# Adding h2 to x2 with a DMA that GpSimd issues, in place of a VectorE instruction, in a two-layer graph network kernel

## The reference

```
h  = relu(layernorm(x))
score = sum(h[src] * h[dst]);  a = softmax of score over the edges of one dst
agg = segment_sum((h @ W_conv + b_conv)[src] * a, dst)
r   = relu(h @ W_res + b_res)
x2  = x + batchnorm(agg + r)                     # layer 1 with its residual
h2 = relu(layernorm(x2))
m  = gelu(gelu([h2[src], h2[dst], edge_attr] @ W_m1 + b_m1) @ W_m2 + b_m2)
boxes = segment_sum(m, dst)
out = x2 + h2 + gelu(gelu([h2, boxes] @ W_c1 + b_c1) @ W_c2 + b_c2)
```

## Time and profile before

| what | value |
|---|---|
| median of 3 runs | 2105.99 us (2104.59 to 2109.98) |
| span of the profiled execution, first to last instruction | 1817.9 us |
| time around the span (median less span) | 288.1 us |
| TensorE busy, in the span | 1463.3 us (80%) |
| VectorE busy | 1485.5 us (82%) |
| GpSimd busy | 1129.4 us (62%) |
| ScalarE busy | 849.3 us (47%) |
| mean granted clock of TensorE | 0.851 of full speed |

### The profile page before, as it was taken

The page is one execution under the profiler, slowest core; times in us unless marked ns, Lnnn a source line. Parts: engine busy times, 40 slices in busy tenths (PEclk is TensorE's granted clock), DMA queues, the critical chain, the costliest instruction groups (busy, mean ns, idle before and its releaser), DMA issues.

```text
span 1817.9 us, 22722 instructions
## 1 busy us (share of the span) xinstructions
PE 1463.3 (80%) x6619; PEld 980.4 (54%) x6619; DVE 1485.5 (82%) x2772; ACT 849.3 (47%) x1497; POOL 1129.4 (62%) x989
## 2 busy tenths in 40 slices
PE   3465556488888888588988988889599999999993
PEld 2133233367777777366656666666345555555541
DVE  8799999688988887798899789888268788788781
ACT  4477777322233222365666566665123433434341
POOL 7777788777777777787500000868756776434446
PEclk9788897667777777797899689888789999999996
DMA  7467664777754333344444434555344453343410
GB/s 232 156 219 229 210 212 157 245 249 261 269 200 130 120 108 110 120 169 159 153 151 165 143 142 163 179 181 174 115 114 146 129 150 106 112 129 101 123 52 17
DMA packets 139616, 286.41 MB, mean 158 GB/s; under 512 B 31154, under 2 KB 48379, under 8 KB 139496
## 3 DMA queue, kind: packets, MB, share of 16 engines
q1 hardware_dynamic: 107176, 254.36, 41.1%
q0 software_dynamic: 32320, 30.62, 7.4%
HBM read 164.51 MB, written 121.80 MB: 157 GB/s over the span
## 4 chain that ended last, share of the span: by engine, by line
PE 48%; DVE 29%; issue 11%; POOL 4%; ACT 4%; DMA 3%; SPq 0%; DVEq 0%; POOLq 0%; ACTq 0%
PE banks L1400 7%; DVE stat L697 5%; PE banks L1390 5%; PE banks L1454 4%; DVE stat L705 4%; PE banks L1321 3%; PE banks L1477 3%; PE banks L1475 3%; PE banks L1484 2%; DVE sums L780 2%; PE banks L1304 2%; DVE xc L711 2%; PE banks L1448 2%; POOL agg_ring L577 2%; PE banks L1372 2%
## 5 line engine op out<-in xcount | busy, mean ns | idle before, releaser
L577 POOL DMA_INDIRECT agg_ring<-agg_rows,edge_idx x196 | 234.6, 1197 | 331.4 <-DMA edge_agg<-agg_ring 270.1
L581 POOL DMA_INDIRECT out<-agg,put_last x196 | 207.6, 1059 | 167.1 <-DVE agg L976 109.9
L577 POOL DMA_INDIRECT x_ring<-in_x,edge_idx x200 | 239.8, 1199 | 63.3 <-issue 60.9
L581 POOL DMA_INDIRECT agg_rows<-agg,put_first x196 | 229.2, 1169 | 59.7 <-issue 57.9
L577 POOL DMA_INDIRECT gout<-in_x,edge_idx x192 | 217.1, 1130 | 58.5 <-issue 57.3
L1400 PEld LDWEIGHTS banks<-packed,cT 96*128 96x128 f32 (+1 forms) x1568 | 202.4, 207 | 43.3 <-issue 42.0
L1400 PE MATMUL banks<-packed,cT 96*128 96x64 f32 (+1 forms) x1568 | 208.8, 291 | 0.0
L1265 PE MATMUL banks<-ident,xc 128*128 128x128 f32 (+1 forms) x784 | 131.4, 316 | 94.1 <-DVE xc L711 94.1
L1265 PEld LDWEIGHTS banks<-ident,xc 128*128 128x128 f32 (+1 forms) x784 | 110.5, 165 | 147.1 <-DVE xc L711 107.7
L1274 PE MATMUL banks<-hT,packed 128*128 128x512 f32 (+1 forms) x196 | 126.8, 781 | 76.3 <-ACT hT L1031 76.3
L1390 PE MATMUL banks<-hT,packed 64*96 64x512 f32 (+1 forms) x392 | 128.5, 735 | 46.4 <-ACT cT L1131 40.8
(11 more groups left out here) (153 smaller groups left out, 3135.9 us busy)
## 6 DMA issues: line engine op xcount, KB each, us to landing
xt<-in_x SPq DMA_DIRECT2D x96, 512.0 KB, 4.2
r_rows<-rT SPq DMA_DIRECT2D x48, 512.0 KB, 5.9
xe<-edge_x SPq DMA_DIRECT2D x96, 256.0 KB, 4.6
agg_rows<-rb SPq DMA_DIRECT2D x48, 512.0 KB
rT<-r_rows SPq DMA_DIRECT2D x48, 512.0 KB, 5.6
out<-xt SPq DMA_DIRECT2D x48, 512.0 KB, 2.6
edge_r<-rr SPq DMA_DIRECT2D x48, 256.0 KB, 3.9
rr<-edge_r SPq DMA_DIRECT2D x48, 256.0 KB, 4.8
```

Source lines behind the costliest of these rows:

```text
L577: A.indirect_dma_start(to, None, table[:, :], bass.IndirectOffsetOnAxis(ap=idx, axis=0), bounds_check=limit, oob_is_err=False).then_inc(si ...
L581: A.indirect_dma_start(table[:, :], bass.IndirectOffsetOnAxis(ap=idx, axis=0), rows_of, None, bounds_check=limit, oob_is_err=False).then_i ...
```

## The change

The VectorE instruction of `add_h2` goes. In its place GpSimd issues, for each step, a plain DMA from SBUF to SBUF that adds: it reads xc and adds it to xt. GpSimd's order is written anew: 36 groups are scattered first; then each step's add is followed by one group, a scatter for the steps 0 to 12 and a gather of group s - 13 from step 13 on. B_y now counts the landings of these DMAs, with three semaphores, one for each buffer of xc. SyncE's schedule of stash_agg follows: up to group a - 14 in the round of pass 3 that has a = 2i, where before it was up to 3 (i - 16).

```diff
+PUTS_AHEAD = 36
-        B_y = stage("x2_plus_h2")
+        B_y = slots("h2_added_to_x2", CS)
...
-                    sp.wait_ge(B_y.sem, B_y.after(S - 1))
+                    B_y.all_done(sp, S)
...
-                due = min(G, max(stashed, 3 * (i - 16)))
+                due = min(G, max(stashed, a - 1 - G + PUTS_AHEAD))
...
+            def add_h2(s):
+                p = nodes_of(s)
+                pool.wait_ge(B_h.sem, B_h.after(s))
+                A.dma_start(xt[s % XS][0:p, :], xc[s % CS][0:p, :], accum_op=ALU.add).then_inc(B_y.of(s), 16)
...
-            for n in range(G):
+            for n in range(PUTS_AHEAD):
                 put_agg(n)
-            G_p.all_done(pool, G)
-            for g in range(G):
+            for s in range(S):
+                add_h2(s)
+                n = PUTS_AHEAD + s
+                if is_group(n):
+                    put_agg(n)
+                if n == G:
+                    G_p.all_done(pool, G)
+                if is_group(n - G):
+                    gather_agg(n - G)
+            for g in range(S + PUTS_AHEAD - G, G):
                 gather_agg(g)
...
-                dve.wait_ge(B_y.sem, B_y.after(s))
+                dve.wait_ge(B_y.of(s), B_y.after(s))
                 V.tensor_tensor(here, here, gout[s % 2][0:p, :], ALU.add).then_inc(B_fin.sem, 1)
-
-            def add_h2(s):
-                p = nodes_of(s)
-                here = xt[s % XS][0:p, :]
-                dve.wait_ge(B_h.sem, B_h.after(s))
-                V.tensor_tensor(here, here, xc[s % CS][0:p, :], ALU.add).then_inc(B_y.sem, 1)
...
-                if a in pair:
-                    add_h2(a)
                 if is_step(a - 1):
                     final_rows(a - 1)
-                if b in pair:
-                    add_h2(b)
```

## The result

The changed kernel took 2019.11 us (median of 4 runs, 2014.78 to 2030.26); the kernel before, beside it, 2107.98 us (4 runs, 2104.59 to 2111.3). The ratio on record is 0.9685, with a 95% interval of 0.9599 to 0.9771: faster by 3.1%. (The two medians divided give 0.958. The record doesn't show how it weighs its ratio.

What follows compares the result with a forecast made beforehand. In pass 3 TensorE and ScalarE pace each round up to L879 of b, VectorE afterwards, with adds covered. 19.9 + 4.0 - 1.0 - 15.1 - 1.6 = +6.2 us on 1817.9, plus 288.1, gives 2112.2 us; range 2092 to 2150.

Steps and rivals of the forecast that it cites:

- With the 288.1 us around it, 2112.2 us: Whole kernel: 288.1 us outside the profiled span added to the forecast span of 1824.1 us gives 2112.2 us.
- the predicted +6.2 us: Whole span: losses at pass 3's start less gains there and at pass 4's start, on 1817.9 us.
- The adds are covered: 0: Rounds of pass 3: VectorE's removed adds, 59.5 us, lie within waits for TensorE's transposes, so removing them gains 0.
- A stall of 19.9 us: Start of pass 3: VectorE waits for the first adding DMA, behind 36 scatter groups; 19.9 us, between 15.8 and 26.0.
- The price of the landing: Each adding DMA of 512 KB: taken to land in 5.7 us, between 2.6 and 11.8.
- The low clock behind it, +4.0 - 1.0: Start of pass 3: one round at TensorE's low clock after the stall, +4.0 us; adds not covered at step 4, -1.0.
- The start of pass 4 gives back 15.1 us: Start of pass 4: earlier gathers and stashes shorten VectorE's 19.52 us mask wait by 15.1 us, between 10 and 19.5.
- The add too late in every round: Rival, pass 3: issue to landing exceeds 11.0 us, VectorE stalls 3.1 us a round, about 2193 us; chance 15%.
- the crowded DMA engines: Rival, pass 3: adds delay the loads of r, costing 1 or 2 us a round, 2136 or 2160 us; chance 8%.
- VectorE as the bound: Rival, pass 3: two adds a round come off the path, 58 us less, 2054 us; chance 5%.

Runs made afterwards that it cites:

- the short kind: Occasions on which all runs of the unchanged kernel before took near 1829 us (1829.13, 1827.16, 1830.77).
- the long kind: Occasions on which all runs of the unchanged kernel before took near 2108 to 2154 us.
- the run meant to show it: Kernel with the new order and VectorE's add: scatters held until pass 2 ends, 36 groups of unread gathers in their places; 1976.46 and 1984.73 us.

## Why the prediction was wrong

**The step that failed is the basis: "With the 288.1 us around it, 2112.2 us", with the profiled execution taken as typical.** A gap of 288 us between a span and its runs is not something that lies around the span (2.1 us do). It said that the profile and the runs were of two kinds. The sum was made for the short kind, and there it was about right: the predicted +6.2 us is 0.3%, and the measured ratio is 1.000, with an interval of 0.45% to either side; span against span, 1819.4 - 1817.9 = +1.5 us. Part of that is luck: the stall and the clock behind it were set 8.9 us too high, and what pass 4 gives back 4.7 us too high, and the two errors mostly cancel. The runs beside it were of the long kind, whose largest cost, the holes, the shown trace doesn't have. With the basis a term failed: GpSimd's order, which the prediction takes as hidden in pass 3 and prices only at its two ends. In the long kind the order alone gives a ratio of 0.9745. No row of the shown trace could have given the size of the holes. But the 288 us could have widened the range, and been a rival of its own.

**What the change gains in the long kind.** It thins GpSimd's back-to-back streams, and in this kind the other engines stand during such streams. How much of the gain comes that way is in part argued. Against the kernel before (span 2161.0) the second run of the changed kernel (2064.6) has -9 us in pass 2, -40 in pass 3, -47 in pass 4, together the 96 us. The order alone has -15, -25 and -47; the adding DMA alone +2, -20 and 0. Pass 2 varies by 30 us between two executions of the changed kernel, so its share is uncertain. Pass 4 is the clearest. In the kernel before the gathers of agg end 158 us into it, and GpSimd then catches up its put_final scatters, one per 1.28 us. The next views show the kernel before, and then the changed one at the same depth in pass 4 (160 and 200 us behind its start):

```profile
1742.00:1782.00 40.00, 30.87 (x88) 15.62 (x88) 17.01 (x39) 7.57 (x13) 30.85 (x31) 0.84 0.29 84
1782.00:1822.00 40.00, 26.23 (x74) 13.47 (x75) 19.88 (x43) 8.71 (x15) 17.33 (x18) 0.68 0.33 102
```

```profile
1693.00:1733.00 40.00, 40.00 (x141) 20.75 (x140) 33.08 (x66) 14.91 (x27) 17.90 (x18) 1.00 0.35 111
1733.00:1773.00 40.00, 40.00 (x144) 21.26 (x143) 33.06 (x66) 15.86 (x29) 17.90 (x18) 1.00 0.36 113
```

TensorE loses 9.1 + 13.8 = 23 us of work in the first pair, runs at 0.84 and 0.68 of its clock, and loses nothing in the second, where the gathers ended 89 us into the pass. In the short kind the kernel before does the same catching up, with GpSimd busy for 31 us of each 40, and TensorE loses nothing; pass 4 there gains only 12 us. In pass 3 the old pace puts three groups of gathers in one round. Where they follow each other without a pause, three of the last six rounds of the kernel before last 27.9, 27.5 and 24.0 us; the changed kernel's last five stay at or below 21.1. That the streams of gathers do this is argued from these rounds only, which make up about half of the 40 us; the run meant to show it fell in the short kind.

**Point by point, in the short kind.**

- *The adds are covered: 0.* Right. Rounds keep their 19.5 and 20.6 us, L893 waits more. The adding DMA alone is no gain in either kind.
- *A stall of 19.9 us.* Right in place and cause, 15.05 us in size, below even the low end of 15.8 (which by its own terms, 781.0 + 1.0 + 2.6 - 768.1, should read 16.5). The first add came at 781.49 (forecast 781.0) and let L719 start 4.9 us later (7.0 had been taken). L719 would itself have begun at 771.4 in that execution, not at 768.1. The price of the landing, taken as 5.7 us, is 6.4 in the median. The Trainium skill's fit (DMA: Bandwidth & Descriptors, Anatomy of one DMA) gave 3.2 us; the fastest landing here took 4.6, so the measurement decides against it for this DMA beside this traffic. The prediction let the adds' issues be held up by VectorE's instructions with two SBUF inputs, up to 2.3 us. They were not: all 49 took 932 to 1057 ns, most of them beside such an instruction. What the scatters showed does not carry over to this DMA. In the long kind there is no stall: pass 3 begins at 954 us, when the 36 groups have long been issued.
- *The low clock behind it, +4.0 - 1.0.* The round with the stall lasts 36.5 us, where the 21.2 of the same round before and the 15.05 of the wait make 36.3; the next ones last 21.1 and 19.5. So no round at the low clock: about 0. Six rounds of the pass take 24.3 us before and six after.
- *The start of pass 4 gives back 15.1 us.* Too much: 19.52 - 11.80 = 7.7. The stashes are queued on SyncE behind the store of the last final rows, and five of them took 18.58 us (forecast: one, and 10.5 us to its landing). Pass 4 as a whole is 12 us shorter, so 4.3 us come on top of the shorter wait, where the prediction had 1.6 for the clock.
- *The rivals.* The add too late in every round, the crowded DMA engines and VectorE as the bound did not occur: L719 waited for the adding DMA 0.6 us in all in the first profile after, at a DMA share of about 0.8. The DMA engines did fill up (900 to 1000 us of short executions: a share of 0.43 before, 0.54 with the order alone, 0.80 with the change), but ScalarE waited for its load only once, 3.2 us. The last three final rows waited for their adds, 10.2 us in all, which the prediction left out; it cost nothing, since before the last two waited 12.2 us for their gelus.

**What stays open.** It stays open why executions come in two kinds, and what it is that holds the engines while GpSimd streams: the trace shows them waiting for nothing that it names, and it holds only half the semaphore records. Open, too, is what makes pass 2 some 70 us longer in the long kind even without scatters, with the gathers of x ending at 642.5 us in place of 581.5. The edit that mends the hole puts in pauses, keeps at most four scatters in flight and so moves 29 groups out of pass 2. Number alone doesn't explain it, as shown above; pauses and the count in flight were not told apart. Nor was it learned whether gathers make such a hole. No version here beats both kernels in both kinds: with spaced scatters the kernel before is 7.1% faster in the long kind and 1.5 to 1.8% slower in the short one; the changed kernel with spaced scatters was not measured in the long kind.

## What to carry to other kernels

Before reading a profile for a forecast, compare its span with the runs. If they differ by much more than the few us that lie around a span, the profile may be of another kind of execution, and the largest cost may not be in it. A stream of indirect DMAs that looks free in one kind of execution, since GpSimd is off the critical path, can go with a stop of every other engine in another: measure it spaced out, by one wait for the group before, ahead of moving work about. And a queue that must first finish a backlog before it serves a new consumer makes that consumer wait for the whole backlog (15 us behind 36 groups of scatters, 103 behind 49 and four groups of gathers).

## What the runs showed of the hardware

- The same kernel took 1829 or 2108 to 2154 us, depending on the occasion, and both kinds came on the same chip; within one occasion the runs of the kernel before agreed within 3%. The traces of the long kind hold about half the semaphore updates of the short one (17,469 against 33,366 for the kernel before).
- In the long kind TensorE, VectorE, ScalarE and SyncE all but stand while GpSimd issues indirect scatters back to back, one per 1.28 us (TensorE busy 17.18 of 140 us), though the DMA engines are busy only 0.11 of the time. With a pause of 2 to 4 us after every fourth scatter TensorE was busy 115.51 of 140. In the short kind TensorE was busy 122.54 of 139 us beside the same back-to-back scatters.
- A DMA from SBUF to SBUF that adds 512 KB costs GpSimd 0.84 to 1.06 us (at most 1.34), also beside VectorE's instructions with two SBUF inputs, where a scatter took 1.63 us. It lands in 6.4 us (4.6 to 10.2) beside other traffic at a DMA share near 0.8.
